# A transformer layer on eight cores: its last gate/up stripe by token groups, part of the quantisation moved into it, and the order of four other waits and loads

## The reference

```python
def _weight_quant(w):
    scale = jnp.clip(jnp.mean(jnp.abs(w)), EPS, None)
    wq = jnp.clip(jnp.round(w / scale), -1.0, 1.0) * scale
def _act_quant(x):
    scale = 127.0 / jnp.clip(jnp.max(jnp.abs(x), axis=-1, keepdims=True), EPS, None)
    xq = jnp.clip(jnp.round(x * scale), -128.0, 127.0) / scale
def _bitlinear(x, w):
    return jnp.einsum('...i,oi->...o', _act_quant(x), _weight_quant(w))
...
x = x + attention(layernorm(x))          # q, k, v, rope, causal softmax, Wo
x = x + ffn(layernorm(x))
# ffn: _bitlinear(silu(_bitlinear(x, w_gate)) * _bitlinear(x, w_up), w_down)
```

## Time and profile before

| | |
|---|---|
| median of 3 runs | 5355.56 us (5346.44 to 5808.53) |
| the profiled execution | 5349.34 us |
| its span, slowest core (3) | 5347.3 us |
| spans of the cores | 5289.0 to 5347.3 us |
| granted TensorE clock, mean of each core | 0.968 to 0.972 |
| busy: TensorE, VectorE, ScalarE, GpSimd | 92%, 58%, 30%, 5% |
| DMA | 916 MB, mean 171 GB/s |

### The profile page before, as it was taken

The page is one execution under the profiler, slowest core; times in us unless marked ns, Lnnn a source line. Parts: engine busy times, 40 slices in busy tenths (PEclk is TensorE's granted clock), DMA queues, the critical chain, the costliest instruction groups (busy, mean ns, idle before and its releaser), DMA issues.

```text
span 5347.3 us, 61904 instructions; the slowest of 8 cores (5289.0 to 5347.3 us)
## 1 busy us (share of the span) xinstructions
PE 4944.2 (92%) x23078; PEld 2225.2 (42%) x23078; DVE 3098.3 (58%) x3773; ACT 1607.0 (30%) x2220; POOL 250.0 (5%) x432
## 2 busy tenths in 40 slices
PE   6989999999688898898899999999999987999999
PEld 3444333333233444443344444444444443444444
DVE  4545666676476666656786676666776646232210
ACT  3421455555365566664111111111111110000000
POOL 0000000000001111211000000000000000000000
PEclk9999999999899999999999999999999988999999
DMA  7667767678655666765664555445554526565543
GB/s 166 164 142 198 181 175 178 172 194 202 129 161 155 182 199 200 231 204 171 173 197 141 176 169 169 151 146 174 172 167 144 161 93 220 172 210 178 190 145 103
DMA packets 473081, 916.45 MB, mean 171 GB/s; under 512 B 137810, under 2 KB 246356, under 8 KB 443988
## 3 DMA queue, kind: packets, MB, share of 16 engines
q1 hardware_dynamic: 372548, 692.23, 43.3%
q0 software_dynamic: 72848, 144.76, 12.0%
q10 hardware_dynamic: 27392, 75.51, 4.6%
HBM read 767.67 MB, written 169.87 MB: 175 GB/s over the span
## 4 chain that ended last, share of the span: by engine, by line
PE 75%; DVE 12%; DMA 8%; ACT 2%; issue 2%; SPq 0%; POOL 0%; ACTq 0%; DVEq 0%; POOLq 0%
PE big L84 36%; PE pb L84 19%; PE p2b L84 16%; DVE p_rinv L84 3%; PE p1b L84 3%; DMA p_R<-wuT 2%; DVE att L84 2%; DVE p_cw L84 1%; DMA att<-vd 1%; DMA p_R<-wgT 1%; DMA p_W<-WvT 1%; DVE p_hst L84 1%; DMA p_wa<-wdT 1%; DMA p_wds<-wdtd 1%; DVE p_lnS L84 1%
## 5 line engine op out<-in xcount | busy, mean ns | idle before, releaser
L84 PE MATMUL big<-p_xiT,p_wgt 128*128 128x512 bf16 x4096 | 927.8, 380 | 7.8 <-DVE p_bst L84 7.8
L84 ACT ACTIVATE att<-big,g_negB 128x1024 bf16<-128x1024 f32 (+3 forms) x640 | 630.7, 985 | 367.6 <-PE big L84 347.1
L84 PEld LDWEIGHTS big<-p_xiT,p_wgt 128*128 128x128 fp8e4 x4096 | 401.0, 98 | 492.7 <-issue 10.9
L84 PE MATMUL big<-p_wds,p_hq 128*128 128x512 fp8e4 x2048 | 447.3, 381 | 43.6 <-DMA p_wds<-wdtd 39.1
L84 PE MATMUL pb<-p_xiT,p_wut 128*128 128x512 bf16 x2048 | 462.9, 379 | 0.0
L84 PE MATMUL p2b<-p_xiT,p_wut 128*128 128x512 bf16 x2048 | 462.9, 379 | 0.0
L84 DVE TENSOR_TENSOR p_hst<-p_hst,p_Fb 128x2048 f32<-128x2048 f32 x64 | 146.7, 2292 | 465.3 <-DMA p_hst<-hd 463.5
L84 PE MATMUL big<-att 128*128 128x512 bf16 (+3 forms) x1280 | 354.6, 360 | 50.7 <-DMA att<-vd 33.3
L84 ACT ACTIVATE p_ab<-p_hb 128x512 f32<-128x512 f32 x256 | 161.4, 630 | 757.9 <-DVE p_hb L84 757.9
L84 PE MATMUL pb<-att 128*128 128x512 bf16 (+3 forms) x1280 | 355.5, 361 | 35.6 <-DVE att L84 35.6
L84 ACT ACTIVATE p_sg<-p_tg 128x512 f32<-128x512 f32 x256 | 161.3, 630 | 690.8 <-DVE p_tg L84 690.8
(11 more groups left out here) (207 smaller groups left out, 5747.9 us busy)
## 6 DMA issues: line engine op xcount, KB each, us to landing
p_R<-wgT SPq DMA_DIRECT2D x128, 512.0 KB, 4.9
p_R<-wuT SPq DMA_DIRECT2D x128, 512.0 KB, 5.0
p_wa<-wdT POOLq DMA_DIRECT2D x256, 256.0 KB, 5.3
hd<-p_hb SPq DMA_DIRECT2D x256, 256.0 KB, 3.7
p_wf<-wdT SPq DMA_DIRECT2D x64, 1024.0 KB, 5.8
p_hst<-hd SPq DMA_DIRECT2D x64, 1024.0 KB, 7.6
p_wds<-wdtd SPq DMA_DIRECT2D x128, 512.0 KB, 4.7
p_wf<-wgT SPq DMA_DIRECT2D x60, 1024.0 KB, 8.3
```

Of the source, the lines that this page charges most:

```text
L84: real = getattr(eng, meth)(*a, **k)
```

## The change

Line numbers are those before.

- K/Q loop: the second `wa_step` at each 16th group goes (765).
- Attention: POOL waits, before each `wo_load`, for ScalarE's work so far. The 256 reductions of w_down and their loads go. A projection's first 15 products wait for the head before the last only, the 16th for the last.
- Scale products: `row_mm` waits for its diagonals and its bank and no longer for all of VectorE; it stands a group later. The first units' banks wait for their own last readers.
- Gate and up: the sum for w_down's mean is made here, 64 activations of 128x2048 with an accumulated sum on ScalarE, at two of three units from unit 12, loads by POOL into two buffers; `mean_down` ends it at unit 110. Down's ternary tiles are made in stripes 7 to 14, eight each.
- The last stripe runs token group by token group. From its sixth unit on, a finished group's maxima are transposed and its scales made (`h_max`, `h_row`, the fourth group's behind down's first 256 products); from its eighth on, each unit also rounds one part of the first group.
- Down: no barrier. `hq` is six parts of four groups in the memory of `xiT`, of the mean's buffers and of the odd stripes' weights; `wds` is four buffers in that of the even ones'. h is loaded by POOL, `wds` by SP. Eight parts of the next token group are rounded during a token group, the other eight at its end, since they overwrite it.

```diff
@@ K/Q loop
                     wa_step()
-                    if i % 16 == 0:
-                        wa_step()
@@ wo_group, mm(c)
+                    if c == NH - 1:
+                        wait(T, ctxdone[(w, NH - 1)])
                     if c == 0:
-                        wait(T, (wsem, wsem.v), ctxdone[(w, NH - 1)])
+                        wait(T, (wsem, wsem.v), ctxdone[(w, NH - 2)])
@@ attention loop
             if g < 64 and g % 4 == 3:
+                wait(G, (sS, sS.v))
                 wo_load(1)
...
-            if g >= 64 and g < len(steps) and steps[g][5][2] is None:
-                npl[0] += 1
-                if npl[0] % 3:
-                    wa_reduce()
-                    wa_load()
@@ scale products
-        def row_mm(bank, free):
-
-            wait(T, (sV, sV.v), hacctok, free)
+        def row_mm(bank, *free):
+
+            wait(T, hacctok, *free)
...
             if g % 4 == 0 and g < 12:
-                gate_cols(g // 4)
+                dtok = gate_cols(g // 4)
             for f in wo_group(3, g, g % 5):
                 f()
-            if g % 4 == 1 and g < 12:
-                row_mm(4 + (g // 4) % 2, (sV, sV.v))
             if g % 4 == 2 and g < 12:
+                row_mm(4 + (g // 4) % 2, dtok, rowfree[(g // 4) % 2])
+            if g % 4 == 3 and g < 12:
                 gate_row(g // 4, 4 + (g // 4) % 2)
@@ down's tiles and mean
-                for ti in range(fw * 4, fw * 4 + 4):
+                for ti in range((fw - 7) * 8, (fw - 6) * 8) if 7 <= fw < 15 else ():
...
+            def mean_sum():
+
+                if wmq:
+                    k, tok = wmq.pop(0)
+                    wait(Sc, tok)
+                    sS.inc(Sc.activation(wmb[k % 2][:], wmb[k % 2][:], AF.Abs,
+                                         accum_out=wmcol[:, k:k + 1]))
+                    wmfree[k % 2] = (sS, sS.v)
+                    mean_load()
@@ banks of the first units
-            bankfree = {b: (sV, sV.v) for b in range(8)}
+            bankfree = {0: wofree[1], 1: wofree[2], 2: wofree[3], 3: wofree[4],
+                        4: rowfree[0], 5: rowfree[1], 6: sumfree[0], 7: wofree[0]}
@@ units
-                if fw == 0:
+                if fw in (0, NFW - 1):
                     units.sort(key=lambda u: u[1])
...
+                        if fw == NFW - 1:
+                            bk = 4 + i % 4
+                            if u >= 5 and u % 4 == 1:
+                                dtok, bankfree[bk] = h_max(u // 4 - 1, bk, bankfree[bk])
+                            if u >= 6 and u % 4 == 2:
+                                bankfree[bk] = h_row(u // 4 - 1, bk, dtok, bankfree[bk])
+                            if u == 3:
+                                wait(G, (sV, sV.v))
+                                for _ in range(3):
+                                    q_load()
+                            if u == 4:
+                                wait(Y, stripefree[0], *[(s, s.v) for s in wsem])
+                                for _ in range(4):
+                                    wd_load()
...
+                        if i == 110:
+                            mean_down(4 + i % 4, bankfree[4 + i % 4])
...
+                        if fw == NFW - 1 and u >= 7:
+                            q_do(last15[(u - 7) // 4])
+                            q_load()
...
+                        if i >= 12 and i % 3 != 2:
+                            mean_sum()
@@ down
-            barrier_all()
...
+            for g in range(9, 16):
+                q_do(last15[g // 4])
+                q_load()
+            for w in range(NW_OWN):
+                if w > 0:
+                    for g in range(8, 16):
+                        q_do(downdone[w - 1])
+                        q_load()
...
+                    if w == 0 and dmc == 0:
+                        dtok, bfree[4] = h_max(3, 4, bfree[4])
+                        bfree[5] = h_row(3, 5, dtok, bfree[5])
+                    if w < NW_OWN - 1:
+                        for _ in range(2):
+                            q_do(*([downdone[w - 1]] if w > 0 else []))
+                            q_load()
```

More of the change, by code:

```diff
@@ L832, in build_program @@
         two = sb2("p2_two", [128, 1024], FP8)
[L833 to L861, removed]
         wsem = dm["w0"]
@@ L1237, in gate_cols @@
             vop("tensor_scalar", colu[:, c], g_sxinv[:, c], swn_u[:], None, ALU.mult)
-            row_prep(colg[:, c])
+            return row_prep(colg[:, c])
+        rowfree = [ctxfree[0], ctxfree[1]]
         xi_load(0)
@@ L1377, in row_max, with hq_of @@
                 abfree[e] = accfree[w] = (sV, sV.v)
+            hqt = [x[:] for x in xiT] + [wm[:].bitcast(BF16), wg1[:].bitcast(BF16)]
+            Fb = Cg
+            lsem = [dm["l0"], dm["l1"], dm["l2"]]
+            lfree = [None] * 3
+            htoks = {}
+            qtok = {}
+            downdone = {}
+            QG = [(w, g) for w in range(NW_OWN) for g in range(16)]
+            ql = []
+            nq = [0]
+            def hq_of(w, g):
+                return hqt[(w * 4 + g // 4) % 6][:, (g % 4) * 2048:(g % 4 + 1) * 2048]
@@ new lines, in h_max @@
+            def h_max(w, bank, free):
+                c = slice(w * 4, w * 4 + 4)
+                wait(T, accfree[w], free)
+                for b in range(4):
+                    tr = T.transpose(pbx[bank][:, b * 128:(b + 1) * 128],
+                                     hacc[:, (w * 4 + b) * 128:(w * 4 + b + 1) * 128],
+                                     identf[:])
+                sT.inc(tr)
+                wait(V, (sT, sT.v))
+                vop("tensor_reduce", hm[:, c], pbx[bank][:].rearrange("p (b k) -> p b k", b=4),
+                    AX.X, ALU.max)
+                btok = (sV, sV.v)
+                vop("tensor_tensor", ha[:, c], hm[:, c], colu[:, c], ALU.mult)
+                vop("tensor_scalar", ha[:, c], ha[:, c], -1.0, 1e-5, ALU.mult, ALU.max)
+                vop("reciprocal", hf[:, c], ha[:, c])
+                vop("tensor_tensor", hf[:, c], hf[:, c], colu[:, c], ALU.mult)
+                vop("tensor_scalar", hf[:, c], hf[:, c], 127.0, None, ALU.mult)
+                vop("tensor_scalar", cd[:, c], ha[:, c], g_rec127[:], swn_d[:], ALU.mult,
+                    ALU.mult)
+                return row_prep(hf[:, c]), btok
@@ new lines, in h_row @@
+            def h_row(w, bank, dtok, free):
+                row_mm(bank, dtok, free)
+                wait(V, (sT, sT.v))
+                vop("tensor_copy", Fb[:, w * 512:(w + 1) * 512], pbx[bank][:])
+                return (sV, sV.v)
+            wdsem = [dm["wd0"], dm["wd1"], dm["wd2"], dm["wd3"]]
+            wds = [wg0[:, i * 4096:(i + 1) * 4096] for i in range(4)]
+            wdfree2 = [None] * 4
+            wq = [(w, dmc, c) for w in range(NW_OWN) for dmc in range(4) for c in range(8)]
@@ L1379, in build_program, with wd_load @@
+            wl = []
+            def wd_load():
+                k = len(wl)
+                if k < len(wq):
+                    w, dmc, c = wq[k]
+                    sl = k % 4
+                    if wdfree2[sl]:
+                        wait(Y, wdfree2[sl])
+                    wdsem[sl].inc(Y.dma_start(wds[sl], d_wdt.ap()[dmc, c]), 16)
+                    wl.append((wdsem[sl], wdsem[sl].v))
             for fw in range(NFW):
@@ L1457, in build_program @@
                 row_max()
-            barrier_all()
+            x1in = [x1b[0][:, i * 512:(i + 1) * 512] for i in range(4)]
+            outb = [x1b[1][:, i * 512:(i + 1) * 512] for i in range(4)]
+            xsem = [dm[f"xi{i}"] for i in range(4)]
+            osem = [dm[f"ob{i}"] for i in range(4)]
+            xfree = [None] * 4
+            ofree = [None] * 4
+            bfree = bankfree
+            wait(Sc, *x1free[0], *x1free[1], *[(s, s.v) for s in x1sem])
+            for g in range(9, 16):
+                q_do(last15[g // 4])
+                q_load()
@@ L1459, in build_program @@
+            wait(Y, *[(o, o.v) for o in osem])
         p4f.close()
+        p4.close()
         p2r.close()
[L1461 to L1606 removed]
```

282 lines of the change are left out of this document (115 added, 167 removed), and 3 rows, old and new, of the table dm.

## The result

| | before | after |
|---|---|---|
| profiled execution, us | 5349.3 | 5141.2 |
| its span, slowest core, us | 5347.3 (core 3) | 5139.6 (core 2) |
| spans of the eight cores, us | 5289.0 to 5347.3 | 5116.5 to 5139.6 |
| TensorE busy, share of the span | 92% | 95% |
| mean granted TensorE clock by core | 0.968 to 0.972 | 0.983 to 0.985 |

Ratio of the times 0.9606, 95% interval 0.9565 to 0.9647: faster, by 3.5 to 4.4%. (In some executions of either kernel one die runs at a lower clock and takes some per cent longer; ratios and profiles leave these out, which is why only cores 4 to 7 are read of experiment 3, while the plain medians of four, 5456 and 5196 us, don't.) The forecast was 5160, its own range 5125 to 5200, and up to 5225 with rivals (a) and (b).

A forecast was written before the change was run, and what follows sets the result against it. TensorE's own stream, 4944 of 5347.3 us, was taken to bound the kernel, only 403 us of standing being winnable. 50 + 27 + 32 + 25 - 2 + 61 = 193 off 5349.3 gave 5156, forecast as 5160 us (5125 to 5200).

The forecast's parts named there:

- (a): K/Q loop: the stops belong to the weight loads, so only 5 of 50 us come: 5205; chance 0.10.
- (b): One set of DMA engines: Wo's loads and down's weights late on any queue; 27 and 38 stay lost: 5225; chance 0.08.
- term 3: Attention: taking out w_down's 256 reductions shortens TensorE's waits for `p_x` and ScalarE's exp; 32 us (20 to 42).
- term 4: Attention's tail: looser waits for last head, scale products and banks start the first gate product earlier; 25 us (15 to 31).
- term 1: K/Q loop: without the second `wa_step`, one step of 3.87 us comes off each stop; 50 us (35 to 58).
- term 2: Attention's first stripe: paced Wo loads fit, barely, between the heads' loads and cut `vd` waits; 27 us (12 to 33).
- Terms 5 and 6: Gate and up: added work covered except `mean_down`, -2 us (0 to -10); last stripe and down: stops go, 61 (50 to 65).
- (c): Gate and up: ScalarE waits for a mean load, Silu behind it; 2% slower at 27.8 us landing, some 5460; chance 0.04.
- (d): TensorE meets VectorE's queue in last stripe and new token stripes, or first stripe's slack goes; 100 us, about 5260; chance 0.06.

The follow-up runs named there:

- experiment 3: Kernel before, only POOL made to wait for ScalarE's latest instruction before each load of a part of Wo; attention's first stripe 129 us (144 before), no ratio.
- experiment 1: Kernel before, only the second `wa_step` of the K/Q loop taken out, all 256 sums still made; ratio 0.992, K/Q 743 us.
- Experiment 2: Kernel before, the second `wa_step` of the K/Q loop kept but moved from `i % 16 == 0` to `i % 16 == 8`; K/Q 749 us.
- experiment 4: Changed kernel without the loads of Wo, its buffer filled with zeros by GpSimd; attention's first stripe 114 us (127 in the changed kernel).
- experiment 7: Kernel before, only the loads of h in down issued by POOL instead of SP; ratio 0.996, down 927.5 us instead of 963.0.
- experiment 8: Changed kernel, the 64 sums for w_down's mean made two a unit in units 12 to 43; gate and up 1921 us, 125 more.

## Where the prediction was right, and where it failed

The total came near; the steps behind it did not. What failed: term 3 put the slow products between attention's stops at nothing, 20 us; term 4 let the wait for VectorE's queue go, where it moved three units on, 10 us; term 1 took core 3 for the kernel and one step off each stop, and named one cause where it takes two; term 2 took "it fits" for "no stop", 10 us.

By the medians the change brought 180.0 us: 33.7 + 17.1 + 55.3 + 25.5 - 21.5 + 69.9. The slowest core gained 207.7. The 28 between them are K/Q: before, the stops scatter over the cores (765 to 811 us, core 3 last), after they don't (740 to 750), and the slowest core counts. How bad they were on the slowest core was partly this execution's: against the 5326 us of the kernel before in its 31 other executions, the gain is 186.

**Term 1, K/Q, 50.** Core 3, on which it was read, gained 69, the middle core 34; both lie outside 35 to 58. Two steps failed. The forecast took core 3 for the kernel and "one step of 3.87 us off each" for the gain; experiment 1 and the stages of core 3 show nearly all stops gone, 36.1 to 2.7 us in the K half. And it posed the cause as either the doubled step or the weight load. Experiment 2 shows for the K half that it is the two together; taking the doubled step out and moving it off the weight load both end the stops. The Q half, which was to tell them apart, could not: there every doubled step falls on a weight load too, and that a load without a doubled step makes no stop only says that the load alone is not enough. The edit was judged rightly all the same, since it removes one.

**Term 2, Wo, 27 (12 to 33).** Measured 17 in the changed kernel, 15 alone. The landing near 10 us was right (8.7); that it ends the stops was not: "it fits, barely" priced throughput, but each head's loads have a deadline, and they are 3.2 us slower with a part of Wo among them (experiment 4).

**Term 3, w_down's sums, 32 (20 to 42).** Measured 55 (56 alone), outside its bounds. The waits were right: `p_x` at 39.7 where 35 stood, `att` at 3.5 where half of 12.7 did, 35 in all. Missing were the 20 us that products between stops cost at the lower clock: the forecast put them at nothing in this term. The forecast had read exactly this after the K/Q stops, 4.80 us where 3.62 is full pace, and left it out of this term, though the stripes' granted clock stood at 0.96. The largest of these stops, before:

```profile
1755.64 1.86 PE L84 MATMUL p2b<-p_Wo,att 128*128 128x512 bf16 x4 [6.00 <-DVE p_x L84]
```

and the busy time of the stretch behind it:

```profile
1755.00:1760.00 5.00, 4.36 (x11) 1.61 (x12) 2.13 (x3) 0.05 (x1) 0.00 (x0) 0.50 0.10 35
```

Four products take 1.86 us where 1.03 is the full pace (3 x 0.2158 and the last one's 0.38), and the granted clock there is 0.50.

**Term 4, tail, 25 (15 to 31).** The first gate product came 25.5 sooner, the third scale product waited 5.84 where 5.6 was worked out (and the second 2.57, which was missed). The failed step is "with the banks' own tokens the 7.8 go". VectorE had 82 us of work for TensorE's 61, and the queue was not shorter for the missing wait: it came due at the next thing that needs its end, `row_mm(3)`, 12.2 us for the 3.0 that stood there before. Net 15, the term's lower end. The forecast had named VectorE's backlog for the third scale product and not followed it to the fourth.

**Terms 5 and 6, gate/up and down, 2 lost and 61 won.** Together 59; measured 69.9 - (21.5 - 10.3) = 58.7. ScalarE's wait for the mean's loads was 0.7 us, `mean_down` 1.2. The inline work came to the 17 it was priced at, but by luck: the forecast took its products at the slow pace they had before, 12.6 us where 7.6 was measured, and waits for the last group alone, 4.4 where 9.6 was measured in all. It is three times 0.60 + 1.05 of TensorE and 1.37 + 1.11 of waits on two of them, and for the last group

```profile
4289.19 2.00 PE L84 MATMUL pb<-p_diag,p_ones 128*128 128x128 f32 x8 [3.57 <-DVE p_diag L84]
4292.27 1.01 PE L84 MATMUL pb<-p_wg,p_xiT 128*128 128x512 fp8e4 x2 [1.08 <-DVE p_Cg L84]
```

with no wait for a quantised group or for weights behind it. Of the gain 35.5 is the queue's (experiment 7); the rest, the dropped barrier and the earlier quantisation, was not run alone. The DMA share rose to 0.73, as said.

**The rivals.** (a) was half right as a mechanism and wrong as a time, since its time had the stops stay when the doubled step goes. (b) is refuted for down's weights by experiment 7, and holds for the 13 us of Wo's that experiment 4 shows. (c): the mechanism is real and its price near the formula (experiment 8), only far away at the pace of the change; whether POOL's descriptors wait for VectorE was not measured. (d) didn't come. So the total was near partly by luck: against the medians terms 1, 2 and 4 were 16, 10 and 10 too high and term 3 23 too low, 193 for 180, and the scatter of the cores that went with the K/Q stops made it 208 in the two executions compared.

## What to carry to other kernels

Price a stop at its length and at the slow products behind it: read the granted clock of the stage, and if it is under 1, the cure of the stops pays more than the stops. When a wait on an engine's whole queue is loosened, ask when that queue is really empty, and put the next thing that needs its end behind that point; else the wait only moves. And read a queue for its order: a load behind one that can't go yet, or behind 26 us of transposes, is late before the DMA engines have seen it.

## What had not been expected of the hardware

- 16 transposing loads hold SP's queue 26.2 us, 1.64 us each, where a plain load of 1 MB right behind them takes it 0.50 to 0.57; everything behind them on SP waits.
- A head's load of 256 KB lands in 4.6 us, and in 7.8 with 512 KB parts of Wo from another queue among them (experiment 4). A block of 512 KB lands in 4.4 to 4.7 us, and in 9.4 to 11.1 beside a weight load (experiment 2).
- Right behind a stop of 6.0 us TensorE's granted clock is 0.50, half of full, and four products take 1.86 us for 1.03 (before, 1755).
- At a DMA share of 0.88 and 252 GB/s (experiment 8, 2600 to 2780) 1 MB loads landed in 7.9 us; in the changed kernel, at 0.68 and 203 GB/s in the same stretch, in 7.3.
